# Attention kernel on one core: the first key tile's scores stand between the third and fourth projection tile of a pair

## The reference

```python
xn = _group_norm(xf, gamma, beta)                       # (8, 512, 1024)
qkv = jnp.einsum('oc,bcl->bol', w_qkv, xn) + b_qkv[None, :, None]
q, k, v = jnp.split(qkv, 3, axis=1)                     # 64 channels a head
weight = jnp.einsum('bct,bcs->bts', q * scale, k * scale)
weight = jax.nn.softmax(weight, axis=-1)
a = jnp.einsum('bts,bcs->bct', weight, v)
hid = jnp.einsum('oc,bcl->bol', w_proj, a.reshape(b, c, L)) + b_proj[None, :, None]
return (xf + hid).reshape(b, c, h, w)
```

## Time and profile before

| | before |
|---|---|
| median of three runs | 2587.29 us |
| the profiled execution | 2586.28 us, span 2584.8 us |
| granted TensorE clock, mean share | 0.992 |
| PE busy with matmuls | 2519.1 us, 97% |
| DVE busy | 1641.7 us, 64% |
| ACT busy | 1052.3 us, 41% |
| POOL busy | 1229.5 us, 48% |
| distance from one `max_turn` to the next, p = 1 of the third batch | 47.79 us |

### The profile page before, as it was taken

The page is one execution under the profiler, slowest core; times in us unless marked ns, Lnnn a source line. Parts: engine busy times, 40 slices in busy tenths (PEclk is TensorE's granted clock), DMA queues, the critical chain, the costliest instruction groups (busy, mean ns, idle before and its releaser), DMA issues.

```text
span 2584.8 us, 36959 instructions
## 1 busy us (share of the span) xinstructions
PE 2519.1 (97%) x12980; PEld 1617.5 (63%) x12980; DVE 1641.7 (64%) x2040; ACT 1052.3 (41%) x1313; POOL 1229.5 (48%) x621
## 2 busy tenths in 40 slices
PE   8999999999799999999999999999999999999997
PEld 6877888888555475556556554755565565557544
DVE  6464555545657756774676577567746765775676
ACT  3332233322344444444454444444444534442443
POOL 3330000000156737755666577377556755771762
PEclk9999999999899999999999999999999999999999
DMA  5331111102212050123023220502230241203001
GB/s 192 135 106 49 49 65 65 64 34 109 104 50 106 17 204 25 82 87 134 25 98 136 75 100 17 204 25 82 90 131 25 98 156 65 82 18 114 17 17 65
DMA packets 64183, 214.14 MB, mean 83 GB/s; under 512 B 9152, under 2 KB 9152, under 8 KB 63168
## 3 DMA queue, kind: packets, MB, share of 16 engines
q1 hardware_dynamic: 49504, 159.41, 16.8%
q0 software_dynamic: 14560, 52.96, 5.6%
HBM read 141.05 MB, written 71.30 MB: 82 GB/s over the span
## 4 chain that ended last, share of the span: by engine, by line
PE 91%; DVE 4%; ACT 2%; POOL 2%; issue 1%; ACTq 0%; DVEq 0%; POOLq 0%
PE psum L1461 17%; PE psum L1214 17%; PE psum L1401 14%; PE psum L1444 13%; PE psum L1411 8%; PE psum L1233 7%; PE psum L1257 4%; PE psum L1285 3%; PE psum L1475 2%; PE psum L1331 1%; POOL a_all L547 1%; PE psum L1225 1%; ACT a_all L756 1%; PE psum L1497 1%; DVE small L1045 1%
## 5 line engine op out<-in xcount | busy, mean ns | idle before, releaser
L547 POOL TENSOR_TENSOR a_all<-a_all 128x1024 f32<-128x1024 f32 x441 | 1053.4, 2389 | 545.8 <-ACT a_all L756 508.0
L1045 DVE TENSOR_REDUCE small<-psum 128x2 f32<-128x1024 f32 x512 | 627.8, 1226 | 322.8 <-PE psum L1411 322.8
L756 ACT ACTIVATE a_all<-psum 128x1024 f32<-128x1024 f32 x512 | 496.6, 1022 | 451.1 <-PE psum L1444 413.6
L1461 PE MATMUL psum<-a_all 128*64 128x512 f32 x2048 | 495.7, 605 | 0.0
L1214 PE MATMUL psum<-r_all 128*128 128x512 f32 x1920 | 454.6, 395 | 16.7 <-DVE small L1045 9.7
L1444 PE MATMUL psum<-r_all 64*128 64x512 f32 x3200 | 426.7, 397 | 4.8 <-ACT a_all L756 2.4
L1214 PEld LDWEIGHTS psum<-r_all 128*128 128x128 f32 x1920 | 359.6, 189 | 107.8 <-DVE small L1045 12.0
L1401 PE MATMUL psum<-r_all 128*128 128x512 f32 x1536 | 371.4, 398 | 5.4 <-DVE r_all L1127 5.4
L1444 PEld LDWEIGHTS psum<-r_all 64*128 64x128 f32 x3200 | 293.7, 185 | 101.2 <-ACT a_all L756 35.8
L1401 PEld LDWEIGHTS psum<-r_all 128*128 128x128 f32 x1536 | 284.1, 189 | 90.5 <-issue 29.9
L1461 PEld LDWEIGHTS psum<-a_all 128*64 128x64 f32 x2048 | 124.3, 136 | 213.6 <-issue 190.6
(11 more groups left out here) (141 smaller groups left out, 2156.4 us busy)
## 6 DMA issues: line engine op xcount, KB each, us to landing
r_all<-w_dram SPq DMA_DIRECT2D x48, 1024.0 KB, 4.9
xn_dram<-a_all POOLq DMA_DIRECT2D x56, 512.0 KB, 4.2
r_all<-xn_dram SPq DMA_DIRECT2D x7, 4096.0 KB, 15.5
a_all<-y_dram SPq DMA_DIRECT2D x9, 2048.0 KB, 7.9
a_all<-x SPq DMA_DIRECT2D x16, 1024.0 KB, 6.3
y_dram<-a_all SPq DMA_DIRECT2D x16, 1024.0 KB, 4.2
out<-a_all SPq DMA_DIRECT2D x32, 512.0 KB, 4.0
w_dram<-a_all POOLq DMA_DIRECT2D x16, 512.0 KB, 3.0
```

What stands on the lines that cost most here:

```text
L547: pool.tensor_tensor(p_sum[:, :, cols], probs[:, 0, :, cols] if i == 1 else p_sum[:, :, cols], probs[:, i % SLOTS, :, cols], ALU.add).then ...
L756: act.activation(probs[:, i % SLOTS, :, cols], psum[half][:, :, :], ACT.Exp, scale=SCALE).then_inc(probs_ready, 1)
L1045: dve.reduce_max(max2[:, :, tile, half], psum[3][:, :, :], AX_X).then_inc(work_free, 2)
L1461: last = pe.matmul(psum[2][h * D:(h + 1) * D, half], v_t[:, i, head], probs[:, i % SLOTS, h, half * HALF:(half + 1) * HALF], start=(i == 0 ...
```

## The change

- Both q tiles leave the work banks: `q_bank(0)` is the first bank of `psum[3]`, `q_bank(1)` the second bank of `psum[2]`, with semaphores `q_full` and `q_free` of their own. `Tally` no longer counts them.
- PE's order: `sums` stands behind `next_qk(1)` instead of `next_qk(2)`. `scores(0)` and the first maximum tile stand between `next_qk(2)` and `next_qk(3)`. A maximum tile stands right behind `next_qk(3)`, and none behind `weigh(7)`. There are still 16.
- ACT: `copy_sums` stands behind projection tile 1 (of p >= 1), and `q_hi` of the fourth tile behind the exponentials of key tile 0.
- DVE: `q_lo` of the fourth tile stands behind reduce 0 and ahead of reduce 1.
- New waits on PE: all of `psum[3]` free ahead of `next_qk(2)`; `q_free[0]` and three HI parts ahead of maximum tile 0; all four HI parts ahead of maximum tile 4; `q_free[1]` ahead of `weigh(0)`.

```diff
@@ -216,6 +216,8 @@
         y_loaded = [sem("y_loaded0"), sem("y_loaded12"), sem("y_loaded3")]
         k_full = [sem("k_full0"), sem("k_full1")]
         k_free = [sem("k_free0"), sem("k_free1")]
+        q_full = [sem("q_full0"), sem("q_full1")]
+        q_free = [sem("q_free0"), sem("q_free1")]
         k_copied = sem("k_copied")
         k_step = sem("k_step")
         v_first_full, v_first_done = sem("v_first_full"), sem("v_first_done")
@@ -264,6 +266,9 @@
         def k_bank(half):
             return psum[2 * half][:, 1 - half]
+        def q_bank(half):
+            return psum[3 - half][:, half]
+
         PAIRS = CT
@@ -274,9 +279,9 @@
         K_STEPS, K_COPIES = 2, 3
-        WORK0 = QK - NH + 2 * MAXES
-
-        NEXT = QK - NH + 2 * MAXES
+        WORK0 = 2 * MAXES
+
+        NEXT = 2 * MAXES
         WORK = PAIRS * NEXT + NT + CT * NH
         assert WORK % 2 == 0 and WORK0 % 2 == 0
@@ -643,12 +648,11 @@
                     act.wait_ge(xn_stored[j % 2], (tb - 1) * STORED + STORED // 2)
                 act.activation(hi_slot[:, j % 2], raw[j], ACT.Copy).then_inc(xn_hi_done, 1)
-            def q_hi(pair, par, i):
+            def q_hi(pair, par, i, made):
                 half = QK_ORDER[i][1]
-                n, ps = work.next()
-                act.wait_ge(work_full, n)
-                act.activation(q_hl[:, par, HI, half * HALF:(half + 1) * HALF], ps, ACT.Identity,
+                act.wait_ge(q_full[half], made + 1)
+                act.activation(q_hl[:, par, HI, half * HALF:(half + 1) * HALF], q_bank(half), ACT.Identity,
                                bias=bqkv_c[:, pair:pair + 1]).then_inc(qk_hi_done, 1)
             def k_copies(pair, i, made):
@@ -676,7 +680,7 @@
                 if QK_ORDER[i][0] == K_OF:
                     k_copies(pair, i, made)
                 else:
-                    q_hi(pair, par, i)
+                    q_hi(pair, par, i, made)
             def copy_sums(b, p):
@@ -716,10 +720,10 @@
                     more = p < PAIRS - 1 or not last
                     par, pairs = (p + 1) % 2, b * PAIRS + p
-                    for i in range(QK):
+                    for i in range(QK - 1):
                         if more:
                             qk_hi((p + 1) % PAIRS, par, i, pairs + 1)
-                        if p and i == 2:
+                        if p and i == 1:
                             copy_sums(b, p - 1)
                         if p >= 2 and i == 2:
                             for h in range(NH):
@@ -755,6 +759,8 @@
                                     act.wait_ge((sum_step, last_sums)[half], (LAST_SUMS, 0)[half] + max(before, 1))
                             act.activation(probs[:, i % SLOTS, :, cols], psum[half][:, :, :], ACT.Exp,
                                            scale=SCALE).then_inc(probs_ready, 1)
+                        if i == 0 and more:
+                            qk_hi((p + 1) % PAIRS, par, QK - 1, pairs + 1)
                         if p and not more and i in (2, 3):
                             hid_hi(b, p - 1, i - 2)
                     if more:
@@ -1008,13 +1014,12 @@
             def q_lo(pair, par, i, made):
-                ps = work.next()[1]
                 half = QK_ORDER[i][1]
                 cols = slice(half * HALF, (half + 1) * HALF)
                 dve.wait_ge(qk_hi_done, made * QK + i + 1)
-                dve.scalar_tensor_tensor(out=q_hl[:, par, LO, cols], in0=ps, scalar=bqkv_c[:, pair:pair + 1],
+                dve.scalar_tensor_tensor(out=q_hl[:, par, LO, cols], in0=q_bank(half), scalar=bqkv_c[:, pair:pair + 1],
                                          in1=f(q_hl[:, par, HI, cols]), op0=ALU.add,
-                                         op1=ALU.subtract).then_inc(work_free, 1)
+                                         op1=ALU.subtract).then_inc(q_free[half], 1)
             def k_steps(par, i, made):
@@ -1151,7 +1156,6 @@
                     if p >= 2:
                         for h in range(NH):
                             hid_lo(b, p - 2, h)
-                    next_qk(3)
                     if p == 0 and stage:
                         dve.wait_ge(xn_hi_done, FIRST_MADE + (b + 1) * CT)
@@ -1163,6 +1167,8 @@
                             dve.wait_ge(max_ready, pairs + 1)
                         for m in range(MAXES):
                             max_tile(m)
+                            if m == 0:
+                                next_qk(3)
                             if p and m % 2:
                                 invert_sums(b, p - 1, m // 2, 1)
                         max_join()
@@ -1394,18 +1400,19 @@
             def qk_tile(slot, i, before=lambda j: None):
                 of, half = QK_ORDER[i]
                 cols = slice(half * HALF, (half + 1) * HALF)
-                to = k_bank(half) if of == K_OF else next_tile()
+                to = (q_bank, k_bank)[of](half)
                 for j in range(CT):
                     before(j)
                     for k, (w, m) in enumerate(THREE):
                         last = pe.matmul(to, w_s[:, slot, of, w, j], xn[:, m, j, cols], start=(j == 0 and k == 0),
                                          stop=(j == CT - 1 and k == 2))
-                last.then_inc(k_full[half] if of == K_OF else work_full, 1)
+                last.then_inc((q_full, k_full)[of][half], 1)
             def max_tile(par, m):
                 half, tile = m // NT, m % NT
                 n = work.next_pair()
-                pe.wait_ge(work_free, n - 2)
+                if work.started or m:
+                    pe.wait_ge(work_free, n - 2)
                 for h in range(2):
                     rows_ = slice(h * D, (h + 1) * D)
                     last = pe.matmul(psum[3][:, h], q_hl[rows_, par, HI, tile * P:(tile + 1) * P],
@@ -1456,6 +1463,7 @@
                         if more:
                             pe.wait_ge(k_free[1], pairs + 2)
+                            pe.wait_ge(q_free[1], pairs + 2)
                     for h in range(2):
                         head = slice((2 * p + h) * D, (2 * p + h + 1) * D)
                         last = pe.matmul(psum[2][h * D:(h + 1) * D, half], v_t[:, i, head],
@@ -1502,6 +1510,7 @@
                         if i == 0 and j == 1:
                             pe.wait_ge(qk_hi_done, QK)
+                            pe.wait_ge(q_free[0], 1)
                         max_tile(0, rows_made)
                         rows_made += 1
             assert rows_made == MAXES
@@ -1524,6 +1533,9 @@
                             if i == 1:
                                 pe.wait_ge(o_ready, ONE + pairs)
+                            if i == 2:
+
+                                pe.wait_ge(work_free, work.upto())
                             qk_tile(p % 2, i)
                     made = [0]
@@ -1533,6 +1545,10 @@
                         made[0] += 1
                         if more:
                             if m == 0:
+
+                                pe.wait_ge(qk_hi_done, (pairs + 2) * QK - 1)
+                                pe.wait_ge(q_free[0], pairs + 2)
+                            if m == NT // NH:
                                 pe.wait_ge(qk_hi_done, (pairs + 2) * QK)
                             max_tile(1 - par, m)
@@ -1543,18 +1559,19 @@
                     if not p:
                         next_qk(0)
                     next_qk(1)
-                    next_qk(2)
                     if p:
                         sums(pairs - 1)
+                    next_qk(2)
+                    scores(pairs, par, 0, more)
+                    next_max()
                     next_qk(3)
-                    for i in range(NT):
+                    next_max()
+                    for i in range(1, NT):
                         scores(pairs, par, i, more)
                         next_max()
-                        if i:
-                            weigh(b, p, i - 1, more)
-                            next_max()
+                        weigh(b, p, i - 1, more)
+                        next_max()
                     weigh(b, p, NT - 1, more)
-                    next_max()
                     assert made[0] == MAXES
                 if last:
                     sums(b * PAIRS + PAIRS - 1, True)
```

## The result

The changed kernel takes 2603.43 us (median of four runs, 2602.38 to 2604.43) against 2587.53 us before: a ratio of 1.0062, 95% interval 1.0044 to 1.0079. It is slower, as forecast, but by 15.9 us where 9.7 were worked out, and 2603.4 lies just outside the range (2582 to 2603). The profiled execution took 2603.35 us, its span 2601.8; the span before was 2584.8.

A forecast was written before the change was run, and what follows sets the result against it. The prediction took PE as the bound (91% of the span). Pairs' starts +20.2, v tiles -10.2 and last pair -0.3 gave +9.7 us on 2586.28, so 2596.0; it gave 2596.5, eight-in-ten range 2582 to 2603.

The forecast's parts named there:

- The hold on DVE: At a pair's start, DVE does `q_lo` of tile 3 before reduce 1, so PE waits 0.97 us at maximum tile 2.
- The distances of PE: Start-to-start times from `next_qk(1)` to `weigh(0)` sum to 16.04 us against 15.03; a pair was taken as 0.65 longer.
- the sentence on p = 0: Pairs with p = 0, 2 and 3 were given the same 0.65 us loss as p = 1.
- 0.4 of room: Ahead of maximum tile 0, the `q_free[0]` wait was to have 0.4 us to spare, so PE would not wait.
- The end: From the last p = 2 turn to the end: +0.35 us; POOL's sooner start makes the last pair's loss 0.3 less.
- The v tiles: At the first v tile behind p = 3, PE's wait goes: 1.46 us seven times, 10.2 us less.
- POOL's room: Between POOL's last add and the sums, about 1.3 us left, some 0.8 behind p = 3; no wait.
- the loop with reciprocals on the other side: In the key-tile loop, reciprocals follow the reduce behind a weighing; they fit the 4.19 us round by 0.13 us, costing nothing.
- weight loads: SP's loads wait for the fourth HI part, 2.4 us later, but serve the pair after the next: no cost.
- the two slower rivals: DVE can't keep up in the loop (2612 us), or the sums wait for POOL (2611 us); chance 0.08 together.
- the new banks win: At a pair's start, q's own banks let `q_lo` lie beside `scores(1)`, reduce 1 not late: 2567 us, chance 0.12.

The follow-up runs named there:

- the doubled `q_lo`: The changed kernel with `q_lo` of tile 3 done twice, first into a scratch buffer, in the 24 pairs of the loop over batches: 2618.1 us.
- the fastest: The changed kernel with `scores(0)` behind tile 3 as before the change, and maximum tile 0 ahead of `scores(0)`: 2576.33 us, ratio to before 0.9961.

## Why the prediction was right in direction and wrong in size

- *The hold on DVE* was the mechanism and was sized right: maximum tile 2 was put 2.78 us behind maximum tile 1, measured 2.77; the doubled `q_lo` agrees. The Trainium skill (VectorE: DVE Perf Modes, The DRAIN you can't avoid) would have the next DVE instruction start only once the pipeline is empty, but adds in the same place, which the prediction leaves out, that one that isn't held starts earlier. The trace agrees with the addition: the doubled one cost 0.66, its pitch, and not the recorded 0.75.
- *The distances of PE* were a little longer. From `next_qk(1)` to `weigh(0)` 16.20 us were measured, 16.04 worked out and 0.07 added. `next_qk(1)` took 2.93 (2.82), tile 3 took 2.94 (2.86), maximum tile 2 to the weighing 0.43 (0.33), and maximum tile 0 to tile 3 0.32 (0.43). Such distances, read between rows of other neighbours, were off by 0.08 to 0.11 each. 16.20 - 15.03 - 0.43 = 0.74 a pair instead of 0.65, and p = 2 lost 0.72. That p = 1 lost only 0.60 is luck of the sum: the kernel before had a third hidden wait there that the prediction overlooked, `scores(2)` took 1.68 us where 1.55 is the rule, and these 0.13 went too.
- *The step that failed* is the sentence on p = 0: "For p = 0 (no sums before or after) and p = 2 and 3 I use the same: the pieces are the same", and with it the "0.4 of room" of `q_free[0]`. The room was worked out as if DVE were free. In p = 1 it is 0.38 as forecast: the sums stand between tiles 1 and 2 and give DVE 1.87 us to finish `k_steps`. In p = 0 there are none, and maximum tile 0 waits. It cost 0.42 us in each of eight pairs (0.31 in front of maximum tile 0, 0.11 behind it, where tile 3 follows at 0.43 instead of 0.32). That is 3.4 of the 7.3 us by which the sum fell short (17.0 against 9.7), and putting `q_lo` one instruction earlier gave them back.
- *The end* was mis-sized by 1.65 us. Into the last pair the sums wait for POOL, 4.4 us now, but up to the last sums the way is only 0.26 longer (87.33 against 87.07). The rest comes behind their start. The stretch from these sums to the first projection matmul (window, length, busy time of PE, PEld, DVE, ACT, POOL, granted clock, DMA share, GB/s), of the kernel before and then of the changed one:

```profile
2549.14:2556.92 7.78, 1.94 (x8) 0.55 (x8) 4.85 (x4) 0.72 (x1) 0.00 (x0) 0.83 0.75 270
```

```profile
2564.47:2573.66 9.19, 3.35 (x8) 0.80 (x8) 4.85 (x4) 0.72 (x1) 0.00 (x0) 0.71 0.61 228
```

  DVE and ACT did the same in both, PE's eight matmuls took 3.35 us instead of 1.94: 1.41 of the 2.0. PE had been idle 3.33 and 3.34 us before them. The eight matmuls alone, before and then after:

```profile
2549.14:2551.08 1.94, 1.94 (x8) 0.55 (x8) 0.00 (x0) 0.00 (x0) 0.00 (x0) 1.00 0.53 78
2564.47:2567.82 3.35, 3.35 (x8) 0.80 (x8) 0.00 (x0) 0.00 (x0) 0.00 (x0) 0.56 0.61 185
```

  The granted clock was 1.00 (its higher level, 2.4 GHz) over all of them before, and 0.56 on the mean in the changed kernel, where it fell to the lower level (1.2 GHz) just behind their start. The changed order isn't enough to bring this: with `q_lo` twice, the same order and the same 4.4 us wait for POOL, the eight took 1.94 again. In the other eight experiments they took 2.74 to 3.68. So the 1.4 us are no cost of the moved blocks that a run here has shown; why the fall comes where it does stays open.
- *The last two batches* account for some 1.7 us of the rest: the kernel before was faster there (47.5 us for p = 1 and 2 instead of 47.7 to 47.8), the changed one not (48.4 to 48.7). Their code stands outside the loop over batches. Two rows of the kernel before, p = 1 of the seventh batch, to be read with the earlier trace rows:

```profile
2192.06 0.39 PE L1411 MATMUL psum<-u,r_all 64*128 64x512 f32 x2
2192.42 1.89 PE L1444 MATMUL psum<-r_all 64*128 64x512 f32 x12
```

  `scores(1)` starts 0.36 behind maximum tile 0 instead of 0.51 (in p = 0, 0.37 instead of 0.65), since ACT starts the first exponential 1.24 us behind `scores(0)` instead of 1.39. The gain lies in the wait for the exponentials, which the changed order doesn't have, so it had nothing to gain there. Why ACT starts sooner stays open.
- *The v tiles, POOL's room, the loop with reciprocals on the other side, weight loads*: as forecast, and neither of the two slower rivals came about. 1.39 us of bracket gone seven times, 0.78 us of POOL's room left of the 0.8 forecast, rounds of 4.19 us, no wait for a load.
- *The rival "the new banks win"* named the right rule for another order. The Trainium skill (Perfetto Trace Analysis, Optimizing Tensor Performance) has matmul groups rotate through PSUM banks so that evacuation lies beside the next group's matmuls. With maximum tile 0 ahead of `scores(0)` the separate banks let maximum tile 0 and `scores(0)` run while tile 3 is still being evacuated, and the kernel is 11 us under the one before. That agrees, but the largest part is the v tiles' wait (1.39 us seven times), and no run has the banks without a new order, so what the banks alone give is not shown. In the changed order the evacuation of the maximum tile stood behind that of another bank in DVE's list.

## What to carry to other kernels

A tile's own bank frees the producer only if the consumer's list lets the evacuations pass in the order in which the producer needs them: put the two lists side by side and look for an instruction that waits for a late input ahead of one whose input is there. Price a moved block for each kind of iteration apart; what stands between two steps in one (here the sums) may be missing in another. A saving at a boundary that comes 7 times (1.46 us here) is not worth a wait of half its size that comes 31 times (0.88 here).

## What the runs showed that I had not expected

POOL, busy 47% of the span, was a bound in waiting. Its adds take about 34 us a pair from the first to the last, and the sums stood 3.8 us behind the last of them in the kernel before (2.0 behind the v tiles), 1.3 (0.8) in the changed one and 0.5 (none) in the fastest. Every tenth saved on PE between `scores(1)` and the sums comes out of this room. That the next gain there has to come from POOL follows only if the sums stay where they are, and no run made POOL faster; with the sums a tile later the room was 3.2 again, and DVE's copies of the v tiles took its place.
